# A decoder layer on one core: where three weight loads of its expert stage stand in SP's queue

## The chip, the cores and the metric

The kernel runs on one core of a Trainium2 chip. The metric is the device time of one execution in microseconds. A core has five engines with a queue each: TensorE (PE; its weight loads are shown as PEld), VectorE (DVE), ScalarE (ACT), GpSimd (POOL) and SyncE (SP), which here does nothing but wait and issue DMAs. Each queue is worked off in order: an instruction that waits on a semaphore holds all that stand behind it on its engine.

## The reference

A batch of 16 sequences of 112 rows of 256 numbers goes through three blocks, each with a residual and a layer norm behind it:

```
x = layernorm(x + ssm(x))        # projection to 512, short convolution, long convolution (FFT in the reference), gate, projection
x = layernorm(x + depool(x, ctx))# rms-norm and projection of x, plus a decayed sum over the first half of ctx
x = layernorm(x + moe(x))        # router: argmax of 8 logits; the chosen expert: relu(x W1.T + b1) W2.T + b2
```

Every row goes to one of eight experts. An expert's first weights W1 (256 x 1024) and its second weights W2 (1024 x 256) are 1 MB each in fp32. The kernel computes no expert that a row did not choose.

## The kernel before

**Stages.** Up to about 78 us the kernel projects, convolves and makes the long convolution's spectrum. From there until about 208 us runs a pipeline over the 16 sequences in 20 steps (`b_steps`: s = 2 * pair + q = 0 to 19). In step s every engine works on several sequences at different lags: `seq(pair, q, lag)` gives the sequence s - lag. Lag 0 loads ctx and x and transforms, lag 1 gates (VectorE) and inverts, lag 2 projects and adds the residual, lag 3 makes x1 and `cross` (the second block), lag 4 makes x2 (rows after the second block), stores it and computes the router's logits. Steps 16 to 19 are the tail in which no new sequence comes in. Behind the pipeline the expert stage runs over tiles of 128 rows sorted by expert, from about 226 us to the end.

**Early tiles.** Three tiles (`EARLY` = 3) don't wait for the whole routing. When the first ten sequences are routed, in step 15, VectorE finds which experts the first three full tiles belong to (`early_experts`, which sets `expert_e_set`) and which rows they hold (`early_tokens`). GpSimd then gathers their rows from `x2_early` with an indirect DMA (`gather_early`, L755): tile 0 in the middle of step 16, tiles 1 and 2 at that step's end. TensorE does the tiles' work between its other work: `turn_early(i)` (L1676) transposes the gathered rows; `hide_early(i, part)` (L1687) is the first product in two halves of 16 matmuls, which needs `w1_e_loaded`; ScalarE applies the relu (`relu_early`, L956); `sum_up_early(i, part)` (L1697) is the second product in two halves of 8 matmuls, which needs `w2_e_loaded` and counts `f_e_ps`. Its order is written by hand: in step 17 project(15), turn_x1(14), turn_x2(13), turn_early(0), cross(14), hide_early(0, 0), logit(13); in step 18 turn_x1(15), hide_early(0, 1), cross(15), sum_up_early(0, 0), turn_x2(14), sum_up_early(0, 1), logit(14), a ranking; in step 19 turn_x2(15), turn_early(1), logit(15), hide_early(1, 0). Tile 1's rest and all of tile 2 follow behind the steps, with the matmuls that place the rows of the main tiles (L1785) between them.

**Weights.** The early tiles have two buffers for either kind of weights: `w1_e` in the region of `w2`, `w2_e` at the start of `stage_b`, in the place of the first two chunks of the gate z, which are free when half the sequences are gated (`gate_set` at 8). Tile 2 uses tile 0's buffers again, so its loads wait until `ht_e_ps` is 2 (first product of tile 0 done) and `f_e_ps` is 1 (second product done). All experts' W1 are loaded into `w1` in 16 pieces of 512 KB: piece n by `load_w1(n, gates)`, which waits until `gates` sequences are gated, since the last pieces lie over the last z chunks. Pieces 0 to 12 go out in steps 0 to 12, pieces 13, 14 and 15 in steps 17, 18 and 19. W2 of experts 0 to 3 goes out in 16 pieces of 256 KB, W2 of experts 4 to 7 behind the steps (L569). `b2`, broadcast to all partitions (1 MB, L560), is needed by VectorE before it copies the first main tile's W1 (`take_w1`, L1400) .

**SP's queue.** All these loads are SP's. In each step it stores x2 of lag 4, loads a W2 piece of lag 1, does what the tail of the function asks, and loads ctx (L536) and x (L538) of lag 0. `load_early_w1` (L503) and `load_early_w2` (L508) first read the tile's expert into a register (`value_load`), then issue. In step 15 both of tile 0 stand last. In step 17 SP waits for all three gathers and then issues both of tile 1 and the next W1 piece. Behind the steps come tile 2's W1, b2, W2 of expert 7, tile 2's W2, and W2 of experts 5, 4 and 6, each with its own wait.

**Main tiles.** GpSimd gathers their rows from `x2_rows` (L788, the first four by 221 us), TensorE transposes them (L1798), ScalarE moves them (L1064), then come 32 matmuls with W1 (L1811) and 16 with W2 (L1830) per tile.

Of the kernel before, what the change touches and what calls it, by code (L numbers as in the profile page):

```python
# [25 lines left out]
NB, L, D = 16, 112, 256  # L26
H, MODES, TAPS = 512, 8, 4
C, PATCHES = 512, 375
NE, FF = 8, 1024
# [15 lines left out]
EARLY, EARLY_SEQS, EARLY_GROUP = 3, 10, 2  # L45
# [61 lines left out]
def need(engine, semaphore, value):  # L107

    if not (isinstance(value, int) and value <= 0):
        engine.wait_ge(semaphore, value)  # L110

def decoder_layer(nc, ins, out):
    at, _ = constant_columns()
    n_const = max(b for _, b in at.values())
    NLAG = LA + LO + 1

    with ExitStack() as ctx:
# [3 lines left out]
        def sem(name):  # L122
            return ctx.enter_context(nc.semaphore(name))
# [105 lines left out]
        def z_chunk(c):  # L229
# [4 lines left out]
        q = Region(stage_b[:, 2 * DT * FF:r.used], r.used - 2 * DT * FF)  # L234
# [18 lines left out]
        q = Region(stage_b[:, late:late + 1848], 1848)  # L253
# [111 lines left out]
        rows_e_loaded = [sem(f"rows_e_loaded{i}") for i in range(EARLY)]  # L365
        rt_e_ps, rt_e_set, ht_e_ps, ht_e_set, f_e_ps, sum_e_set = (
            sem(s) for s in ("rt_e_ps", "rt_e_set", "ht_e_ps", "ht_e_set", "f_e_ps", "sum_e_set"))
# [8 lines left out]
        def b_steps(engine, step):  # L376

            for s in range(NB + EPI):
                step(s // 2, s % 2)

        def seq(pair, q, lag):

            par, half = (q - lag) % 2, pair + (q - lag) // 2
            b = 2 * half + par
            if isinstance(b, int) and not 0 <= b < NB:
                return None, par, half
            return b, par, half
# [39 lines left out]
        def apart(engine, *waits):  # L427

            waits = [(s, v if isinstance(v, int) else engine.snap(v)) for s, v in waits]  # L430
            if not all(isinstance(v, int) for _, v in waits):
                engine.wait_ge(loaded["consts"], 16)
            for s, v in waits:
                need(engine, s, v)
# [25 lines left out]
        @block.sync  # L460
        def _(sp):
            sp.dma_start(lens, ins["lens"]).then_inc(loaded["lens"], 16)
            sp.dma_start(consts[:, 0:n_early], ins["consts"][:, 0:n_early]).then_inc(loaded["consts_early"], 16)

            def load_w_in(h):
                sp.dma_start(w_in[:, :, h * P:(h + 1) * P], ins["w_in"][:, :, h * P:(h + 1) * P])\
                  .then_inc(w_in_loaded[h], 16)

            def load_hid(c):
                sp.dma_start(hid_t[:, :, c * CW:(c + 1) * CW], ins["x_t"][:, :, c * CW:(c + 1) * CW])\  # L470
                  .then_inc(hid_loaded[c], 16)

            load_w_in(0)
            load_hid(0)
            for h in range(1, HT):
                load_w_in(h)
            sp.dma_start(w_in[:, :, H:2 * H], ins["w_in"][:, :, H:2 * H]).then_inc(loaded["w_in_z"], 16)
            for c in range(1, NC):
                load_hid(c)
            sp.dma_start(consts[:, n_early:], ins["consts"][:, n_early:]).then_inc(loaded["consts"], 16)  # L480
            sp.dma_start(w_out, ins["w_out"]).then_inc(loaded["w_out"], 16)
            for dst, name in ((w_x[:, :, :], "w_x"), (g_res[:, :], "g_res"), (w_r[:, :, :], "w_r"),
                              (b1[:, :], "b1"),
                              (u[L:L + 1, 0, :], "b_x"), (u[L:L + 1, 1, :], "b_x"),
                              (decay[L:L + 1, :], "one_row")):
                sp.dma_start(dst, ins[name]).then_inc(loaded["small"], 16)
            sp.dma_start(b_r[:, :], ins["b_r"].to_broadcast([L, NE])).then_inc(loaded["small"], 16)
            sp.dma_start(g_init[:, :], ins["g_init"].to_broadcast([L, D])).then_inc(loaded["small"], 16)

            sp.wait_ge(pad_set, 1)  # L490
            sp.dma_start(x2_rows[T:T + 1, :], pad_row).then_inc(loaded["pad"], 16)
            sp.dma_start(x2_early[EARLY_SEQS * L:EARLY_SEQS * L + 1, :], pad_row).then_inc(loaded["pad"], 16)
            def load_w1(n, gates):

                need(sp, gate_set, gates)
                sp.dma_start(w1[:, n // 2, n % 2, :], ins["w1"][:, n // 2, n % 2, :]).then_inc(loaded["w1"], 16)

            w2_pieces = ins["w2"].rearrange("p e m d -> p (e m d)")

            def load_early_w1(i):  # L500

                e = sp.value_load(expert_e[0:1, i:i + 1], min_val=0, max_val=NE - 1)
                sp.dma_start(w1_e[i % 2], ins["w1"][:, e, :, :]).then_inc(w1_e_loaded[i % 2], 16)  # L503

            def load_early_w2(i):

                e = sp.value_load(expert_e[0:1, i:i + 1], min_val=0, max_val=NE - 1)
                sp.dma_start(w2_e[i % 2], ins["w2"][:, e, :, :]).then_inc(w2_e_loaded[i % 2], 16)  # L508

            def step(pair, q):  # L510

                b, par, half = seq(pair, q, 4)
                if b is not None:
                    sp.wait_ge(x2_set, b + 1)
                    sp.dma_start(x2_rows[bass.ds(b * L, L), :], x2[:, par, :]).then_inc(x2_stored[par], 16)
                    if b < EARLY_SEQS:
                        sp.dma_start(x2_early[bass.ds(b * L, L), :], x2[:, par, :]).then_inc(early_stored[par], 16)

                b, par, half = seq(pair, q, 1)
                if b is not None:  # L520
                    sp.wait_ge(dft_ps, b + 1)
                    sp.dma_start(w2_flat[:, bass.ds(b * H, H)], w2_pieces[:, bass.ds(b * H, H)])\
                      .then_inc(loaded["w2"], 16)
                if 2 * pair + q == NB + 1:
                    for i in range(EARLY):
                        sp.wait_ge(rows_e_loaded[i], 16)
                    load_early_w1(1)
                    load_early_w2(1)
                if 2 * pair + q > NB:
                    load_w1(2 * pair + q - 4, NB)  # L530
                b, par, half = seq(pair, q, 0)
                if b is None:
                    return
                need(sp, u_set, b - 1)
                need(sp, sq_set, b - 1)
                sp.dma_start(ctx_sb[:, par, :], ins["ctx"][b, :, :]).then_inc(c_loaded[par], 16)  # L536
                need(sp, pre_set, b - 1)
                sp.dma_start(x_res[:, par, :], ins["x"][b, :, :]).then_inc(x_loaded[par], 16)  # L538
                if isinstance(b, int) and b == 0:
                    sp.wait_ge(spec_set, HT)  # L540
                    sp.wait_ge(xt_ps, HT * NC)
                    sp.wait_ge(loaded["pad"], 32)
                if b >= PRO:
                    sp.wait_ge(decay_set, 1)
                if b <= 12:
                    load_w1(b, 10 if b == 12 else 0)
                if b == NB - 1:
                    sp.wait_ge(expert_e_set, 1)
                    sp.wait_ge(gate_set, NB // 2)
                    sp.wait_ge(z_ps, UNITS)  # L550
                    load_early_w1(0)
                    load_early_w2(0)

            b_steps(sp, step)
            sp.wait_ge(out_ps, NB)
            sp.wait_ge(gate_set, NB)
            sp.wait_ge(cross_ps, NB)
            sp.wait_ge(ht_e_ps, 2)
            load_early_w1(2)
            sp.dma_start(shared[:, :], ins["b2"].to_broadcast([P, NE * D])).then_inc(loaded["b2"], 16)  # L560
            for e in (7, 5, 4, 6):
                if e == 5:
                    sp.wait_ge(f_e_ps, 1)
                    load_early_w2(2)
                if e in (4, 5):
                    sp.wait_ge(ht_e_ps, 6 if e == 4 else 4)
                if e == 6:
                    sp.wait_ge(rows_loaded[0], 16)
                sp.dma_start(w2[:, e, :, :], ins["w2"][:, e, :, :]).then_inc(loaded["w2"], 16)  # L569
# [1319 lines left out]
```

## Time and profile before

| | |
|---|---|
| median of three runs | 348.27 us (347.13 to 348.81) |
| the profiled execution | 348.85 us, span 347.0 us |
| TensorE busy | 324.0 us, 93% of the span |
| VectorE, GpSimd, ScalarE busy | 213.0, 200.3, 151.2 us |
| granted TensorE clock, mean | 0.981 of full |
| DMA | 42.43 MB, mean 122 GB/s |

A row of the timeline gives an instruction's start from the span's begin, its length, its engine, its line and what it writes and reads; a bracket gives the idle time of the engine before it and what ended that. The chain of the work that ended last gives, for each piece, the time for which it alone decided when the rest could go on: for a DMA it counts from the issue.
### The profile page before, as it was taken

The page shows a single profiled execution, that of the slowest core. Times are in us where ns is not written, and L with a number is a line of the kernel's source. Part 1 is how long each engine was busy: PE and PEld are TensorE (multiplying, and loading weights), DVE is VectorE, ACT ScalarE, POOL GpSimd, SP SyncE. Part 2 cuts the span into 40 slices and gives each one's busy share as a digit, 9 for nine tenths or more (in the row PEclk, how much of TensorE's full clock was granted, in tenths as well). Part 3 has the DMA queues.
Part 4 walks back from the last instruction along what each step waited for, and adds up shares of the span by engine and source line. Part 5 has one row for each costly group of instructions (what it writes and reads, how often), then busy time and mean ns, then how long its engine had stood idle before and what let it go on. Part 6 is the DMA issues. An engine that isn't in the chain of part 4 may idle for free.

```text
span 347.0 us, 6576 instructions
## 1 busy us (share of the span) xinstructions
PE 324.0 (93%) x1923; PEld 255.3 (74%) x1924; DVE 213.0 (61%) x497; ACT 151.2 (44%) x383; POOL 200.3 (58%) x325
## 2 busy tenths in 40 slices
PE   7999989999999999999996899889999999999970
PEld 2555555567777778777784788789999999999950
DVE  5999994625977788788886246543344444354431
ACT  3888864246543444443354333233432234422320
POOL 4689990335587685786867221412764565565552
PEclk9999999999999999999999699999999999999996
DMA  6910002503357665576338679940110101110120
GB/s 186 363 43 2 2 0 62 161 0 107 125 173 235 192 190 158 183 208 176 89 86 297 220 265 376 347 201 8 69 50 28 33 30 29 32 33 30 30 48 24
DMA packets 19999, 42.43 MB, mean 122 GB/s; under 512 B 3761, under 2 KB 10905, under 8 KB 18554
## 3 DMA queue, kind: packets, MB, share of 16 engines
q1 hardware_dynamic: 17370, 37.32, 32.8%
q0 software_dynamic: 1872, 4.59, 4.7%
q8 instruction: 17, 0.28, 0.4%
q14 instruction: 20, 0.16, 0.2%
q10 hardware_dynamic: 720, 0.08, 0.2%
HBM read 37.16 MB, written 5.34 MB: 122 GB/s over the span
## 4 chain that ended last, share of the span: by engine, by line
PE 72%; DVE 14%; DMA 6%; POOL 2%; issue 2%; ACT 1%; SPq 1%; ACTq 1%; DVEq 0%; POOLq 0%
PE ps L1811 16%; PE ps L1830 15%; DVE stage_b L1126 9%; PE ps L1609 7%; PE ps L1631 7%; PE ps L1498 5%; PE ps L1547 4%; PE ps L1654 4%; DMA stage_b<-in_w 4%; PE ps L1548 4%; DMA early<-x_early,early 2%; PE ps L1658 2%; PE ps L1687 1%; PE ps L1697 1%; PE ps L1666 1%
## 5 line engine op out<-in xcount | busy, mean ns | idle before, releaser
L1811 PEld LDWEIGHTS ps<-stage_b 128*128 128x128 f32 x480 | 55.8, 192 | 2.3 <-issue 1.6
L1811 PE MATMUL ps<-stage_b 128*128 128x128 f32 x480 | 56.2, 275 | 1.2 <-ACT stage_b L1064 1.2
L1830 PE MATMUL ps<-w,stage_b 128*128 x240 | 54.4, 380 | 0.9 <-DVE stage_b L1437 0.9
L1830 PEld LDWEIGHTS ps<-w,stage_b 128*128 128x128 f32 x240 | 44.4, 190 | 6.7 <-issue 1.3
L1278 DVE TENSOR_TENSOR stage_b<-ps,w 112x512 f32<-112x512 f32 x64 | 39.7, 682 | 13.6 <-PE ps L1548 11.5
L718 POOL TENSOR_TENSOR stage_b<-stage_b 112x512 f32<-112x512 f32 x16 | 21.4, 1336 | 37.8 <-DVE stage_b L1278 25.6
L1609 PEld LDWEIGHTS ps<-consts,stage_b 112*128 112x128 f32 x256 | 31.0, 192 | 7.3 <-issue 6.6
L1055 ACT ACTIVATE stage_b<-ps,b 128x128 f32<-128x128 f32 x120 | 32.7, 383 | 5.6 <-issue 5.6
L1064 ACT ACTIVATE stage_b<-ps 128x256 f32<-128x256 f32 x16 | 6.1, 384 | 65.8 <-PE ps L1798 65.8
L788 POOL DMA_INDIRECT stage_b<-x_rows,stage_b x18 | 28.3, 1571 | 7.3 <-issue 5.2
L1126 DVE SCALAR_TENSOR_TENSOR stage_b<-ps,w,stage_b 128x444 f32<-128x444 f32 (+2 forms) x48 | 31.1, 671 | 1.1
L1609 PE MATMUL ps<-consts,stage_b 112*128 112x112 f32 x256 | 31.1, 274 | 0.1
L1631 PE MATMUL ps<-w,stage_b 128*112 128x256 f32 x128 | 30.3, 380 | 0.0
L1400 DVE COPY stage_b<-w 128x2048 f32 x16 | 19.8, 1238 | 15.0 <-issue 11.4
L1461 PE MATMUL ps<-w 128*128 128x448 f32 x64 | 26.6, 543 | 0.9 <-DMA w<-in_x_t 0.9
L966 ACT ACTIVATE stage_b<-stage_b 112x256 f32<-112x256 f32 x16 | 9.6, 599 | 40.5 <-POOL stage_b L737 40.5
L1498 PE MATMUL ps<-w 128*128 128x448 f32 x64 | 26.7, 544 | 0.0
L1437 DVE TENSOR_TENSOR stage_b<-ps,shared 128x256 f32<-128x256 f32 x15 | 6.4, 424 | 29.6 <-PE ps L1830 28.9
L1631 PEld LDWEIGHTS ps<-w,stage_b 128*112 128x112 f32 x128 | 21.3, 177 | 3.8
L719 POOL TENSOR_TENSOR stage_b<-stage_b 112x512 f32<-112x512 f32 x16 | 20.7, 1292 | 0.0
L834 POOL DMA_INDIRECT out<-stage_b x15 | 15.8, 1052 | 8.4 <-POOL stage_b L831 8.4
L1165 DVE TENSOR_SCALAR stage_b<-stage_b 128x256 f32<-128x256 f32 x15 | 6.2, 412 | 21.4 <-POOL stage_b L829 21.4
(217 smaller groups left out, 599.4 us busy)
## 6 DMA issues: line engine op xcount, KB each, us to landing
w<-in_w SPq DMA_DIRECT2D x16, 512.0 KB, 4.5
w<-in_w SPq DMA_DIRECT2D x7, 1024.0 KB, 4.8
w<-in_w SPq DMA_DIRECT2D x16, 256.0 KB
stage_b<-in_ctx SPq DMA_DIRECT2D x16, 224.0 KB, 3.1
stage_b<-in_w SPq DMA_DIRECT2D x3, 1024.0 KB, 7.3
w<-in_x_t SPq DMA_DIRECT2D x4, 448.0 KB, 6.3
stage_b<-in_x SPq DMA_DIRECT2D x16, 112.0 KB, 2.9
x_rows<-stage_b SPq DMA_DIRECT2D x16, 112.0 KB
```

The source lines that it names most:

```text
L718: g.tensor_tensor(y_spec[:, 0, :], prod[:, 0, :], prod[:, 1, :], ALU.subtract)
L719: g.tensor_tensor(y_spec[:, 1, :], prod[:, 2, :], prod[:, 3, :], ALU.add).then_inc(y_set, 1)
L788: g.indirect_dma_start(rows[:, place, :], None, x2_rows, bass.IndirectOffsetOnAxis(ap=index, axis=0)).then_inc(rows_loaded[place], 16)
L1055: last = a.activation(h_t[:, par, m * P:(m + 1) * P], ps[:, 2 * par + m // 4, (m % 4) * P:(m % 4 + 1) * P], ACT.Relu, bias=b1[:, bass.ds(e ...
L1126: ins_ = v.scalar_tensor_tensor(acc[:, :, back:L], raw[:, :, 0:L - back], conv_w[:, h, tap:tap + 1], acc[:, :, back:L], ALU.mult, ALU.add)
L1278: last = v.tensor_tensor(prod[:, n, :], ps[0:L, x_part, :], spec[:, k_part, :], ALU.mult)
L1461: last_ = m.matmul(ps[:, h, 0:CW], w_in[:, k, h * P:(h + 1) * P], hid_t[:, k, bass.ds(c * CW, CW)], start=(k == 0), stop=(k == DT - 1))
L1498: last_ = m.matmul(ps[:, z_bank(unit), 0:CW], w_in[:, k, H + unit % HT * P:H + (unit % HT + 1) * P], hid_t[:, k, unit // HT * CW:(unit // ...
L1609: last_ = m.matmul(ps[:, 3, h * L:(h + 1) * L], y_spec[:, s, h * P:(h + 1) * P], const(name, L), start=(s == 0), stop=(s == 1))
L1631: last_ = m.matmul(ps[0:L, 4, 0:D], gated[:, par, h * L:(h + 1) * L], w_out[:, h, :], start=(h == 0), stop=(h == HT - 1))
L1811: last_ = m.matmul(ps[:, 2 * par + f // 4, (f % 4) * P:(f % 4 + 1) * P], w1_now[par][:, k, f * P:(f + 1) * P], rows_t[:, par, k * P:(k + 1 ...
L1830: last_ = m.matmul(ps[:, 4 + par, 0:D], h_t[:, par, f * P:(f + 1) * P], w2[:, e, f, :], start=(f == 0), stop=(f == FT - 1))
```

## The change

Three things in SP's queue, and nothing on another engine.

- The second weights of early tile 0 no longer go out in step 15, right behind its first weights. They go out in step 16, behind the W2 piece, after a wait until tile 0's gather has landed. In step 17 SP accordingly waits for the gathers of tiles 1 and 2 only.
- Pieces 13 and 14 of W1 go out in steps 14 and 15, behind the W2 piece and ahead of ctx, with waits until 12 and 14 sequences are gated. In step 17 only piece 15 is left.
- Behind the steps, the second weights of tile 2 go out right behind its first weights, ahead of b2 and of W2 of expert 7; before, both stood ahead of them.

```diff
--- before.py
+++ after.py
@@ -521,13 +521,17 @@
                     sp.wait_ge(dft_ps, b + 1)
                     sp.dma_start(w2_flat[:, bass.ds(b * H, H)], w2_pieces[:, bass.ds(b * H, H)])\
                       .then_inc(loaded["w2"], 16)
+                    if 13 <= b < 15:
+                        load_w1(b, 2 * (b - 7))
+                if 2 * pair + q == NB:
+                    sp.wait_ge(rows_e_loaded[0], 16)
+                    load_early_w2(0)
                 if 2 * pair + q == NB + 1:
-                    for i in range(EARLY):
+                    for i in range(1, EARLY):
                         sp.wait_ge(rows_e_loaded[i], 16)
                     load_early_w1(1)
                     load_early_w2(1)
-                if 2 * pair + q > NB:
-                    load_w1(2 * pair + q - 4, NB)
+                    load_w1(2 * NE - 1, NB)
                 b, par, half = seq(pair, q, 0)
                 if b is None:
                     return
@@ -549,7 +553,6 @@
                     sp.wait_ge(gate_set, NB // 2)
                     sp.wait_ge(z_ps, UNITS)
                     load_early_w1(0)
-                    load_early_w2(0)
 
             b_steps(sp, step)
             sp.wait_ge(out_ps, NB)
@@ -557,11 +560,10 @@
             sp.wait_ge(cross_ps, NB)
             sp.wait_ge(ht_e_ps, 2)
             load_early_w1(2)
+            sp.wait_ge(f_e_ps, 1)
+            load_early_w2(2)
             sp.dma_start(shared[:, :], ins["b2"].to_broadcast([P, NE * D])).then_inc(loaded["b2"], 16)
             for e in (7, 5, 4, 6):
-                if e == 5:
-                    sp.wait_ge(f_e_ps, 1)
-                    load_early_w2(2)
                 if e in (4, 5):
                     sp.wait_ge(ht_e_ps, 6 if e == 4 else 4)
                 if e == 6:
```

## Rows read from the trace of the kernel before

**Rows 1.** The page: its first line and the chain by engine.
```profile
span 347.0 us, 6576 instructions
...
PE 72%; DVE 14%; DMA 6%; POOL 2%; issue 2%; ACT 1%; SPq 1%; ACTq 1%; DVEq 0%; POOLq 0%
```

**Rows 2.** The chain that ended last, in order: start us, us, what.
```profile
184.56 7.48 DMA early<-x_early,early
...
192.78 1.71 PE ps L1654 x4
194.49 0.85 PE ps L1658 x2
195.34 2.85 PE ps L1687 x16
...
198.74 1.80 PE ps L1687 x16
200.54 0.86 PE ps L1654 x4
...
208.67 12.97 DMA stage_b<-in_w
```

**Rows 3.** TensorE in time: start, us, line, operation, count [idle before <-releaser].
```profile
189.06 0.41 PE L1642 MATMUL ps<-consts,stage_b 112*128 112x112 f32 x2 [0.75 <-ACT stage_b L1039]
192.09 0.69 PE L1676 MATMUL ps<-consts,early 128*128 128x128 f32 x2 [2.62 <-DMA early<-x_early,early]
...
221.69 3.72 PE L1697 MATMUL ps<-stage_b 128*128 128x256 f32 x16 [1.73 <-DMA stage_b<-in_w]
```

**Rows 4.** Stretches: length, busy us (count) of five engines, TensorE clock, DMA share, GB/s.
```profile
188.00:190.00 2.00, 0.72 (x4) 0.30 (x4) 0.36 (x2) 1.80 (x5) 1.44 (x4) 1.00 0.98 345
190.00:192.00 2.00, 0.00 (x0) 0.00 (x0) 0.00 (x0) 0.00 (x0) 1.79 (x4) 0.66 0.87 316
220.00:222.00 2.00, 0.32 (x1) 0.30 (x2) 1.58 (x5) 1.14 (x4) 1.46 (x3) 1.00 1.08 416
```

**Rows 5.** SP in time: its DMA issues around the change.
```profile
176.79 0.31 SPq L536 DMA_DIRECT2D stage_b<-in_ctx  x1
...
182.39 0.38 SPq L503 DMA_DIRECT2D w<-in_w  x1
183.54 0.36 SPq L508 DMA_DIRECT2D stage_b<-in_w  x1
...
194.34 0.34 SPq L503 DMA_DIRECT2D w<-in_w  x1
...
206.61 0.35 SPq L503 DMA_DIRECT2D w<-in_w  x1
...
208.67 0.35 SPq L508 DMA_DIRECT2D stage_b<-in_w  x1
```

**Rows 6.** Landings of L503, of L755 (without its first), of L788, in this order.
```profile
DMA to landing us min/median/max: 4.6/4.8/6.8
...
DMA to landing us min/median/max: 3.6/4.2/4.7
...
DMA to landing us min/median/max: 3.6/4.0/7.8
```

**Rows 7.** GpSimd in time: the third early gather, r1, the first main gather.
```profile
189.92 0.95 POOL L755 DMA_INDIRECT early<-x_early,early  x1 [0.30 <-issue]
...
192.00 0.26 POOL L737 TENSOR_SCALAR stage_b<-stage_b 112x2 f32<-112x2 f32 x1
...
216.10 1.09 POOL L788 DMA_INDIRECT stage_b<-x_rows,stage_b  x1 [1.88 <-DVE stage_b L1383]
```

**Rows 8.** ScalarE in time: the ctx square of sequence 15, a relu of tile 2.
```profile
182.12 0.61 ACT L981 ACTIVATE stage_b<-stage_b 112x512 bf16<-112x512 f32 x1
...
220.60 1.14 ACT L956 ACTIVATE stage_b<-ps,b 128x128 f32<-128x128 f32 x4 [1.15 <-PE ps L1687]
```

**Rows 9.** VectorE in time: the first copy of a main tile's first weights.
```profile
218.21 1.27 DVE L1400 COPY stage_b<-w 128x2048 f32 x1 [1.05 <-issue]
```

## The prediction

> **What bounds the kernel now.** The profiled execution took 348.85 us for a span of 347.0 [rows 1], so 1.85 us lie around the span; the median of the three runs is 348.27, 0.58 below it. I take the saving from the span and subtract it from the median. I read four views in this order. First the chain that ended last: TensorE holds 72% of it, and only two of its pieces behind the start are transfers: the gather of early tile 0's rows, 7.48 us from its issue at 184.56, and the load of early tile 2's second weights, 12.97 us from 208.67 [rows 2]. Second, TensorE in order of time, to see how much of each transfer it really waits: 2.62 us ahead of the turn of tile 0's rows at 192.09, and 1.73 us ahead of tile 2's second product at 221.69 [rows 3]. Most of either transfer is hidden; the two idle pieces are what a better order can give. Third, the stretches: TensorE's clock was 1.00 (2.4 GHz) from 188 to 190 and 0.66 from 190 to 192, while it stood idle [rows 4]. The chain shows what followed: four matmuls of `cross` took 1.71 us where they take 0.86 eight microseconds on, the next two 0.85, half a first product of an early tile 2.85 against 1.80 [rows 2]. So the wait is paid twice, once as idleness and once as 1.2 GHz. Fourth, SP's queue and the landings, for who can be early.
>
> **Part 1: tile 0's second weights load behind its gather.** Before, SP issued the first weights at 182.39 and the second at 183.54, 1 MB each, and the gather followed at 184.56 [rows 5, 2]. It took 7.48 us; the next two gathers, the second issued at 189.92, when that traffic was running out, took 3.6 to 4.7, and the main gathers have a median of 4.0 [rows 6, 7]. From 184 on the engines moved about 345 GB/s [rows 4]. Ahead of the gather's end stood 1.05 (first weights) + 1.05 (second) + 0.115 (x2 store) + 0.262 (w2 piece) + 0.131 (the gather) = 2.61 MB, 7.6 us at that rate, from about 183.9 (1.5 us behind the first issue) to 191.5; the trace has 192.04. Without the second weights 1.56 MB remain, 4.5 us, so it ends at 188.4, and with the same 0.5 us of excess at 188.9. The shortest gather, 3.6 us, gives 188.2 [rows 6]. TensorE reaches the turn when the two transposes at 189.06, 0.41 us long, are through, at 189.47 [rows 3]. So the gather stops being awaited: 2.62 us saved, with 0.6 to 1.3 us in hand. Bounds: 0 if the gather stays at 7.48, 2.62 if it lands by 189.47; no gain beyond that, since the transposes ahead of it wait for ScalarE.
>
> The clock: the two short idle pieces before 189.47 stay, but they stood there with the clock at 1.00, and a 1.73 us wait later left 220 to 222 at 1.00 too, with TensorE busy 0.32 of 2 us [rows 3, 4]. I therefore take the clock to stay up. The saving is (1.71 - 0.86) + (2.85 - 1.80) = 1.90, and half of what ran at half clock and has no twin here, 0.85 and the turn's 0.69: 0.77. In all 2.67 us; bounds 0 and 2.67.
>
> What is late next: x1 of sequence 15 waits for GpSimd's r1 at 192.00 + 0.26 [rows 7] and one ScalarE pass of 0.6, so its turn can start at 192.9. In the shifted order TensorE needs it at 189.47 + 0.3 + 0.86 + 0.43 + 1.80 + 0.2 = 193.1. That just fits: 0 to 0.3 us lost, 0.1 taken.
>
> Then the moved load itself. SP waits until 188.9, needs 0.8 us to read the expert (the gap of 1.15 us between its issues at 182.39 and 183.54 less the first one's 0.38), and issues at 189.7. With a landing of 4.8 us for the shortest loads of this size, plus 0.26 MB of gathers in the same stretch (0.8 us), it lands at 195.3 [rows 5, 6]. It is first used behind the second `cross`, which ended at 200.54 + 0.86 + 0.43 = 201.8, in the new time 201.8 - 5.2 = 196.6 [rows 2]. 1.3 us in hand; cost 0. Its range is a landing of 4.6 to 12.97 us, 194.3 to 202.7, so 0 to 6.1 us.
>
> Queued behind SP's new wait are the x2 store of sequence 13 (its buffer is next wanted for sequence 15, two steps on), then the waits for gathers 1 and 2 and tile 1's weights. Gather 2, issued 189.92, now shares its time with the moved 1 MB: 4.7 + half of 2.9 = about 6, so 195.9 instead of 193.6, and tile 1's first weights go out at 196.6 instead of 194.34 and land at 201.4 [rows 5 to 7]. TensorE wants them at 207.4 before, 202.2 now. 0.8 us in hand; I take 0.2 us for it, range 0 to 3.
>
> **Part 2: two pieces of the late first weights in steps 14 and 15.** 512 KB each go out ahead of the ctx load of their step, on gates that VectorE set a step earlier. Each costs SP one issue of about 0.4 us and ctx about 0.52/0.345 = 1.5 us. The ctx load issued at 176.79 would land at 181.9 if I give it the 3.6 us of the shortest transfer in rows 6 and the piece ahead; ScalarE squares it at 182.12 [rows 5, 6, 8]. 0.2 us in hand: cost 0, range 0 to 1. What they take away are two of three such pieces from 194 to 206, 1.05 MB of traffic or 3 us of the queue. This covers the extra megabyte that Part 1 moves there.
>
> **Part 3: tile 2's second weights ahead of b2 and w2[7].** Before: first weights 206.61, b2, w2[7], second weights 208.67, landed 221.64 [rows 5, 2]. Now their wait (tile 0's product done) is met before 206.6, so they are second in line instead of fourth: 2.1 MB less ahead, 5 to 6 us. The wait of 1.73 us goes. What is late next is ScalarE's second half of the relu, 220.60 + 1.14 = 221.74 before [rows 8]; TensorE is free at 219.96 (221.69 less its wait), and the first half of the 3.72 us product takes it to 221.8 as well. Saving 1.7 us; bounds 0 and 1.8. The price is b2, one megabyte (2.9 us) later; VectorE's first weight copy at 218.21 stands behind it [rows 9]. It ends at 219.5 and is wanted when the product of 221.69 is through, 225.4 before and, on the same axis, 223.7 now, so 4.2 us cover it. The main tiles' first gather, issued at 216.10 into a full queue [rows 7], has landed by about 223 (an estimate from its 6.8 us; the longest of these is 7.8 [rows 6]) and was wanted at 225.4. Shifted by 5.2 it lands at 217.7 to 218.7 and is wanted at 218.5: 0 to 0.2 us lost, 0.1 taken.
>
> The main tiles behind are TensorE's own work, one product after the other, and shift as they are.
>
> **Sum.** 2.62 + 2.67 + 1.7 = 6.99, less 0.1 + 0.2 + 0.1: 6.6 us. 348.27 - 6.6 = 341.7 us (the profiled execution: 342.3).
>
> The row against which a rule can be held is the 7.48 us gather [rows 2]. The Trainium skill ("DMA: Bandwidth & Descriptors", Queues, rings and completion order) says that each DMA engine takes turns between the queues it has work for, a packet at a time. By that rule the gather, on its own queue, would hardly stand behind SP's second megabyte, and taking it away would win little; the sum would be Part 3 alone, 346.6. The same section says that a semaphore's increment lands only after the earlier writes of its engine in all queues, which fits the row.
>
> **Rivals.** (a) The gather is late anyway: it reads rows just stored and takes 7.48 for a reason other than the queue. For: it is the first of its kind, and it overlaps the first weights too. Against: 3.6 to 4.7 for the next two, 7.8 only where the queue is full again. Part 1 gives nothing: 348.27 - 1.7 = 346.6. (b) The clock falls nonetheless, on the short idle pieces before 189.47 (one of 0.75 us, one like it). Against: it had not fallen by 190. 6.6 - 2.67 = 3.9 saved, 344.4. (c) SP's wait makes tile 1's weights late. If gather 2 takes 7.5 us, it lands at 197.4, the first weights go out at 198.2 and land at 203.0 to 205.0, and TensorE idles 0.8 to 2.8 us: 1.6 more than I charge, 343.3; with the clock down as well 345.9. (d) Slower: the moved load is late itself. TensorE stands ahead of tile 0's second product, in the middle of the last steps, with the turn of x2 14 behind it. With the 12.97 us of the third such load it would land at 202.7, 6.1 us late, and 2.7 more go to the clock: 6.6 - 8.8 = 2.2 slower, 350.5. It decides from a landing at 200.5, 10.8 us behind the issue. For: that row. Against: that load had some 3 MB ahead of it, this one has 0.26.
>
> **How the numbers follow.** Forecast 0.66, with its own range 340.5 to 343.2; (a) 0.09, (b) 0.08, (c) 0.12, (d) 0.03, something unforeseen 0.02. The range 340.4 to 345.4 leaves out (a), (d), the clock case of (c) and the tails of the forecast, about 2 in 10. About 0.5% (1.7 us) is what can be told from no change. (a) lies on that bound and is shared between same and faster: faster 0.90, same 0.06, slower 0.04.
>
> **What would show it.** Right: the gather at 184.56 lands before 189.4; L1676 has no idle time; the clock is 1.00 from 186 to 235; L1687's first half 1.8 us; the second weights are issued near 189.7; L1697 at about 215 follows L1687 without a DMA as releaser; the first L1811 starts near 219.5. Wrong: the gather over 5 us, the clock below 1 after 190, or a DMA as the releaser of L1687 or L1697.

## The result, and the profile after

The changed kernel takes 344.64 us (343.41 to 345.29, 4 runs) against 348.23 (347.13 to 348.81): 3.6 us less, ratio 0.9889, interval 0.9852 to 0.9925. Run again over five rounds it takes 342.60 against 348.33, ratio 0.9851 (0.9815 to 0.9887). The ratios leave out the slow executions, and they can differ by up to 0.003 from the quotient of the two medians. The forecast was 341.7, its range 340.4 to 345.4: the first median is 2.9 us above the forecast and inside the range.

The profiled execution has a span of 343.4 us, 3.6 less than before. First the chain that ended last, of the changed kernel; these rows answer to [rows 2].

```profile
186.09 5.26 DMA early<-x_early,early
...
191.39 0.69 PE ps L1678 x2
192.08 1.71 PE ps L1656 x4
193.79 0.85 PE ps L1660 x2
194.64 1.94 PE ps L1689 x16
...
197.13 1.80 PE ps L1689 x16
198.93 0.86 PE ps L1656 x4
...
218.36 3.46 PE ps L1699 x16
...
222.66 3.81 PE ps L1813 x32
```

The gather takes 5.26 us instead of 7.48. No load stands in the chain behind it: the 12.97 us piece ahead of tile 2's second product is gone. But `cross` still takes 1.71 us, as before, and the half of the first product behind it 1.94, where it was 2.85 before and the other half takes 1.80: TensorE ran at half clock again, for a shorter time. The stretches, with TensorE's, its loads', VectorE's, ScalarE's and GpSimd's busy us, the clock, the DMA share and GB/s, show when; they answer to [rows 4].

```profile
188.00:190.00 2.00, 1.20 (x6) 0.54 (x4) 1.30 (x4) 1.17 (x3) 1.61 (x5) 1.00 0.70 266
190.00:192.00 2.00, 1.02 (x5) 0.81 (x6) 0.00 (x0) 1.38 (x4) 1.65 (x2) 0.86 0.17 42
192.00:194.00 2.00, 2.00 (x6) 1.43 (x5) 0.00 (x0) 0.58 (x2) 1.57 (x4) 0.50 0.55 115
194.00:196.00 2.00, 2.00 (x15) 1.90 (x14) 1.03 (x3) 1.18 (x3) 0.14 (x1) 0.79 0.96 387
```

TensorE in order of time shows what is left of the two waits of [rows 3].

```profile
190.57 0.41 PE L1644 MATMUL ps<-consts,stage_b 112*128 112x112 f32 x2 [0.74 <-ACT stage_b L1041]
191.39 0.69 PE L1678 MATMUL ps<-consts,early 128*128 128x128 f32 x2 [0.41 <-DMA early<-x_early,early]
...
218.19 3.62 PE L1699 MATMUL ps<-stage_b 128*128 128x256 f32 x16
```

2.62 us became 0.41 and 1.73 became nothing. From the gather's issue to the first product of the main tiles it was 226.25 - 184.56 = 41.69 us and is 222.66 - 186.09 = 36.57: 5.12 us gained. Of these 2.2 are the idleness ahead of the turn (7.53 to 5.30 us behind the issue) and 2.0 lie at tile 2's second product: its wait of 1.73 and 0.26 of the product behind it (3.72 against 3.46 in the chain). The remaining 0.9 is the clock: from the turn to tile 1's first product it was 15.31 us before and is 14.40 now, and 12.76 in the profile of the changed kernel below in which the clock stayed up, so 2.6 were lost before and 1.6 now. The span shows only 3.6, since the gather was issued 1.53 us later than before. That delay is from the kernel's first matmuls, which the change does not touch. TensorE in time, before and then after:

```profile
7.21 3.27 PE L1461 MATMUL ps<-w 128*128 128x448 f32 x8 [0.92 <-DMA w<-in_x_t]
...
7.05 4.97 PE L1463 MATMUL ps<-w 128*128 128x448 f32 x8 [1.98 <-DMA w<-in_x_t]
```

The same eight matmuls took 1.70 us longer, and this is the clock once more: from 8 to 10 us it was 1.00 before and 0.50 here. In the repeated profile of the same kernel they take 3.27 again and the gather's issue is at 184.22, earlier than before's. The change has no part in it, and the time from the gather's issue to the first main product leaves it out. This measure is used below for every profile, beside the times.

### The profile page after: what moved, and what is told of

Read it like the earlier page. It is cut to its first block, busy times and chain, and to the rows that moved or that the text cites. A ratio compares the mean times of both kernels' runs of the same rounds, so it can differ in the third digit from the quotient of the medians.

```text
span 343.4 us, 6576 instructions
## 1 busy us (share of the span) xinstructions
PE 323.3 (94%) x1923; PEld 255.1 (74%) x1924; DVE 213.0 (62%) x497; ACT 151.1 (44%) x383; POOL 199.9 (58%) x325
## 4 chain that ended last, share of the span: by engine, by line
PE 78%; DVE 11%; DMA 4%; ACT 2%; POOL 2%; issue 1%; SPq 0%; DVEq 0%; POOLq 0%; ACTq 0%
PE ps L1813 16%; PE ps L1832 14%; DVE stage_b L1128 8%; PE ps L1611 7%; PE ps L1633 7%; PE ps L1500 5%; PE ps L1549 4%; PE ps L1656 4%; PE ps L1550 4%; PE ps L1689 3%; PE ps L1699 3%; PE ps L1660 2%; DMA early<-x_early,early 2%; PE ps L1463 1%; DMA w<-in_x_t 1%; PE ps L1668 1%
## 5 line engine op out<-in xcount | busy, mean ns | idle before, releaser
L1463 PE MATMUL ps<-w 128*128 128x448 f32 x64 | 28.3, 572 | 2.0 <-DMA w<-in_x_t 2.0
L1500 PE MATMUL ps<-w 128*128 128x448 f32 x64 | 26.7, 544 | 0.0
```

The costliest lines, as they stand in the source:

```text
L1463: last_ = m.matmul(ps[:, h, 0:CW], w_in[:, k, h * P:(h + 1) * P], hid_t[:, k, bass.ds(c * CW, CW)], start=(k == 0), stop=(k == DT - 1))
L1500: last_ = m.matmul(ps[:, z_bank(unit), 0:CW], w_in[:, k, H + unit % HT * P:H + (unit % HT + 1) * P], hid_t[:, k, unit // HT * CW:(unit // ...
```

## The experiments

| kernel | ratio (95%) | issue to first main product, gain |
|---|---|---|
| changed, first measurement | 0.9889 (0.9852 to 0.9925) | 36.57 us, 5.1 |
| changed, again | 0.9851 (0.9815 to 0.9887) | 35.07, 6.6 |
| part 3 alone (e1) | 0.9974 (0.9946 to 1.0003) | 39.11, 2.6 |
| part 1 alone (e2) | 0.9973 (0.9937 to 1.0010) | 37.09, 4.6 |
| part 2 alone (e3) | 0.9959 (0.9931 to 0.9986) | 39.73, 2.0 |
| before, pauses filled (e6) | 0.9925 (0.9892 to 0.9959) | 43.00, -1.3 |
| changed, pauses filled (e5) | 0.9841 (0.9791 to 0.9891) | 34.87, 6.8 |
| changed, w2 piece behind (e4) | 0.9825 (0.9770 to 0.9880) | 34.66, 7.0 |
| changed, first weights behind too (e9) | one run, 345.50 us | 38.62, 3.1 |
| without part 2 (e8) | 0.9842 (0.9786 to 0.9899) | 36.49, 5.2 |
| without part 3 (e10) | 0.9866 (0.9809 to 0.9923) | 37.11, 4.6 |
| e4 and piece 15 last (e11) | 0.9799 (0.9747 to 0.9850) | 34.43, 7.3 |
| e11, pauses filled (e12) | 0.9787 (0.9738 to 0.9836) | 34.43, 7.3 |

The kernel before spread over 346.3 to 352.1 us in these rounds, so half a per cent between two of these kernels is not told apart by their times; the right column is one execution each. Changed again and e1 to e3 ran on one chip, e4, e5, e6 and e9 on a second, e8 and e10 to e12 on a third, each beside the kernel before.

**The changed kernel again.**

> The changed kernel once more, beside its parts. Theory: from the gather's issue on it gains 5.1 us (2.2 of idleness ahead of L1678, 1.0 of the clock, 1.8 of the second product of tile 2), and the 1.5 us by which its start was longer in the first profile is chance: over five rounds it comes out 4.5 to 5.2 us faster (ratio 0.985 to 0.987). Rival: the later start belongs to the change; then 3.3 to 3.9 us (0.989 to 0.9905).

Within the stated times. This execution went as the forecast had it. TensorE in time:

```profile
189.01 0.44 PE L1678 MATMUL ps<-consts,early 128*128 128x128 f32 x2
189.28 1.06 PE L1656 MATMUL ps<-w_x,stage_b 128*112 128x256 f32 x4
190.61 1.95 PE L1689 MATMUL ps<-stage_b,w 128*128 128x128 f32 x16
...
209.81 0.57 PE L1787 MATMUL ps<-stage_b,w 112*128 112x42 bf16 x16 [0.48 <-POOL stage_b L778]
```

The gather landed in 4.7 us, before L1678 wanted it, nothing waited, the clock stayed at 1.00 and `cross` and the first product ran at full speed. 5.3 us were gained up to tile 1's first product (17.55 us behind the gather's issue, 22.84 before); then 0.65 was given back, at a place that the forecast did not name. VectorE shows it:

```profile
206.53 0.17 DVE L1369 TENSOR_SCALAR stage_b<-ps 128x8 f32<-128x8 f32 x1 [1.07 <-DMA x_rows<-stage_b]
```

Before it computes the main tiles' rows, VectorE waits for the store of the last x2. With everything 5 us earlier, that store stands behind tile 1's two loads and piece 15 in SP's queue; with piece 15 behind the store (e11, below) the wait is gone.

**Its three parts alone.** Part 3: only the tail's order, as in the change's last two hunks. Part 1: only

```diff
                     load_early_w1(0)
-                    load_early_w2(0)
...
+                if 2 * pair + q == NB:
+                    sp.wait_ge(rows_e_loaded[0], 16)
+                    load_early_w2(0)
                 if 2 * pair + q == NB + 1:
-                    for i in range(EARLY):
+                    for i in range(1, EARLY):
```

and part 2: only the lines with `load_w1`.

> Only part 3: tile 2's second weights ahead of b2 and of W2 of expert 7. Theory: the parts add up, and this one is worth its wait of 1.73 us: 1.6 to 1.9 us faster (0.9945 to 0.9955), the gather unchanged at about 7.5 us and the clock at half from about 191 to 196. Rival: the queue of that stretch is full whatever the order, and w2[7] or the main gather becomes late instead: under 0.8 us.

> Only part 1: tile 0's second weights behind its gather, with the first weights' pieces 13 to 15 and the tail order as before. Theory: the gather lands in about 5.3 us, L1676 waits 0.4 us and the clock still falls for some 4 us: 3.2 us faster (0.990 to 0.992). If part 2 is needed to make room for the moved megabyte, tile 1's weights or L1697 wait here and it is under 2.5 us.

> Only part 2: pieces 13 and 14 of the first weights in steps 14 and 15. Theory: nothing waits for these pieces and ctx lands in time, so same time within 0.4 us (0.999 to 1.001). Rival: they clear the queue for tile 2's second weights (which would then land earlier, since less traffic stands before 206) and bring up to 1 us, or they delay ctx of sequence 15 and cost up to 1 us.

Part 3's trace is as expected (tile 2's second product follows the first with no wait); its time has room for the expected 1.6 us, but for nothing as well. The other two theories failed. Part 2 is worth 1.4 us, not nothing: its rival, the queue cleared for tile 2's second weights, is what came, and for more than the 1 us that I gave it. Here is TensorE in time with part 2 alone, tile 2's second product:

```profile
218.11 3.81 PE L1689 MATMUL ps<-stage_b,w 128*128 128x128 f32 x32 [0.52 <-issue]
221.75 3.62 PE L1699 MATMUL ps<-stage_b 128*128 128x256 f32 x16
```

The 1.73 us wait is gone although tile 2's weights still stand fourth in line. So parts 2 and 3 remove the same wait, and I had credited it to part 3 only. Part 1 alone came out 0.9 us faster, an interval that includes no change, where its profile has 4.6; its runs spread from 343.95 to 352.15. In the profiled execution, the fastest of them, TensorE in time still has the other wait:

```profile
189.80 0.44 PE L1678 MATMUL ps<-consts,early 128*128 128x128 f32 x2 [0.65 <-DMA early<-x_early,early]
190.07 1.03 PE L1656 MATMUL ps<-w_x,stage_b 128*112 128x256 f32 x4
...
216.78 3.72 PE L1699 MATMUL ps<-stage_b 128*128 128x256 f32 x16 [1.69 <-DMA stage_b<-in_w]
```

What this kernel's other executions wait for, no profile shows. The times of the three parts (0.9, 0.9 and 1.4 us) add up to less than the whole change gained, the profiles (2.6, 4.6 and 2.0) to more than it did. That parts 2 and 3 overlap is shown by the wait that either removes, not by the times.

**The clock by itself.** In both kernels constants are multiplied in TensorE's pauses ahead of the turn of tile 0; their results are not used and overwritten.

```diff
+            def keep_busy(n):
+                pe.wait_ge(prod_set, NB)
+                for _ in range(n):
+                    m.matmul(ps[:, 0, :].rearrange("p (r n) -> p r n", r=4), ones16[:, :], filler, start=True, stop=True)
...
                     project(NB - 1)
+                    keep_busy(2)
                     turn_x1(NB - 2)
+                    keep_busy(3)
                     turn_x2(NB - 3)
+                    keep_busy(11)      # 1 in the changed kernel
                     turn_early(0)
```

> The kernel before, with 16 matmuls of constants (128x512, bf16, results not used) in TensorE's three pauses ahead of the turn of tile 0: two, three and eleven. No transfer changes, so the gather still takes 7.5 us and L1676 still starts 7.5 us behind its issue. Theory: the clock falls only because TensorE stands idle; kept busy it stays at 1.00, cross takes 0.86 and the first half product 1.80, and the kernel is 2.6 to 2.8 us faster (0.992 to 0.9925) with the wait itself still there. Rival: the clock falls for another reason, or the turn starts late behind the fillers: no gain or slower.

> The changed kernel with six such matmuls in the same three pauses (two, three and one; together 1.3 of the 1.8 us of idleness). Theory: the short pauses together with the 0.4 us wait are what lets the clock fall; filled, it stays at 1.00, cross 0.86, first half product 1.80: 1.6 to 1.8 us faster than the changed kernel, so 6.2 to 6.9 us against before (0.980 to 0.982). Rival: the clock level is decided further back, gain under 0.5 us over the changed kernel.

Before, filled, is 0.75% faster, 2.6 us (0.9892 to 0.9959), as expected, with no transfer moved and the gather at 7.52 us. TensorE in time of this kernel:

```profile
189.36 2.54 PE L1683 MATMUL ps<-ones 128*128 128x512 bf16 x11
192.19 0.44 PE L1676 MATMUL ps<-consts,early 128*128 128x128 f32 x2 [0.29 <-DMA early<-x_early,early]
192.47 1.03 PE L1654 MATMUL ps<-w_x,stage_b 128*112 128x256 f32 x4
193.77 1.95 PE L1693 MATMUL ps<-stage_b,w 128*128 128x128 f32 x16
...
221.38 5.41 PE L1703 MATMUL ps<-stage_b 128*128 128x256 f32 x16 [3.90 <-DMA stage_b<-in_w]
```

The turn starts no earlier, but behind it everything runs at full speed: tile 1's first product starts 12.73 us behind the turn, 15.31 before. That is the clock's share of the wait, measured alone, 2.6 us. The last row is why this one execution, at 350.27 us above its kernel's median of 346.59, was no faster: tile 2's weights, issued at 206.34, 2.3 us earlier than before, landed 15 us later, at 221.34, where they had landed at 221.64 before, and the product behind them took 5.41 us, not 3.72. When TensorE comes earlier the tail's loads become the bound; parts 2 and 3 are for this. In the changed kernel the fillers kept the clock at 1.00 too, but the expected 1.6 to 1.8 us over the unfilled one did not come: 0.9841 is not to be told from 0.9851. The profile of the unfilled one had the clock at 1.00 as well the second time.

**What the gather's length depends on.** One kernel moves the last 256 KB piece of the second weights behind the gather too, the other tile 0's first weights.

```diff
                     sp.wait_ge(dft_ps, b + 1)
+                    if b == NB - 1:
+                        sp.wait_ge(rows_e_loaded[0], 16)
+                        load_early_w2(0)
                     sp.dma_start(w2_flat...
```

```diff
                     sp.wait_ge(z_ps, UNITS)
-                    load_early_w1(0)
...
                     sp.wait_ge(rows_e_loaded[0], 16)
+                    load_early_w1(0)
                     load_early_w2(0)
```

> The changed kernel with the last 256 KB piece of the second weights also behind the gather. Theory: the gather lands when what stands ahead of it in the queues has drained, so it comes 0.5 to 0.7 us earlier (4.6 us), the 0.41 us wait of L1678 goes, and the clock falls less or not at all: 0.4 us faster than the changed kernel, up to 2.2 if the clock stays up. Rival: the gather takes 5.3 us for reasons of its own (its 128 rows, the x2 store): same time as the changed kernel.

> The changed kernel with tile 0's first weights behind the gather as well, so that only the x2 store and one 256 KB piece are in flight with it. Theory: the gather lands in 3.6 to 3.9 us; then TensorE waits for the first weights instead (issued at about 190.5, landed at 195 or later, wanted at 191) and the kernel is slower than the changed one. Rival: the gather's length does not come from SP's traffic: still about 5.2 us.

Without the first weights the chain reads

```profile
184.29 3.07 DMA early<-x_early,early
...
188.33 4.77 DMA w<-in_w
```

So the gather takes 3.07 us with 0.4 MB of SP's in flight, 3.4 to 4.5 with the first weights and the store (e4, e11, e12), 4.2 to 5.5 with the 256 KB piece besides (the changed kernel, e2, e5, e8, e10), and 7.05 to 7.52 with both megabytes (before, e1, e3, e6). It grows with what SP has ahead of it, though the two middle groups overlap; a reason of its own, my rival (a), is out.

The two later gathers show how late a load can still hold one up. In ten cases SP issued a megabyte of weights shortly behind such a gather's issue. Where it did so 0.8 to 1.3 us behind, the gather took 2.8 to 3.7 us (e2, e5, e11, e12), 0.65 us behind, 4.0 and 4.1 (the changed kernel, e10), and 0.1 to 0.3 us behind, 5.2 to 6.1 (changed again, e4, e8, e9). GpSimd is busy with the issue for 0.95 to 1.08 us, so such a load may still get ahead of part of the gather; that reason is not shown.

As expected, the kernel that moves both now waits for the first weights, 2.30 us (345.5 us, one run, which does not order it by time). The piece moved behind takes the gather off TensorE's path, at 3.4 us where 4.6 was expected, and has the lowest ratio of the single edits to the changed kernel, though not clear of it.

**Without part 2, without part 3.** The change less the `load_w1` lines, and the change less the tail's hunks.

> The change without part 2 (pieces 13 to 15 of the first weights in steps 17 to 19 as before). Theory: either part 2 or part 3 alone takes the 1.7 us wait of tile 2's second product away, but behind part 1 the queue of 195 to 215 is full, so the megabyte of the two pieces comes back as late landings: the x2 store of sequence 15 or tile 2's weights are waited for 0.5 to 2 us more than in the changed kernel, 3.0 to 4.7 us faster than before (0.9865 to 0.9915), and scattered. Rival: part 3 alone is enough, same time as the changed kernel (0.985).

> The change without part 3 (tile 2's second weights behind b2 and W2 of expert 7 as before). Theory: with tiles coming 5 us earlier, two megabytes more ahead of this load make L1699 wait 1 us or more: 3.0 to 4.3 us faster than before (0.9875 to 0.9915). Rival: the pieces out of the way are enough, as they were alone; same time as the changed kernel (0.985).

Without part 2 the time is the rival's, without part 3 it lies between theory and rival; in either case part 1 with one other part is within the scatter of the whole change. Both profiled executions gained less than the changed kernel's second one. Tile 2's second product starts 0.3 us late in the one without part 3 (3.92 us behind its first, against 3.64), not the 1 us or more of the theory. And in both the clock fell. In the one without part 2 the turn started 0.49 us behind the transposes ahead of it, against 0.31 in the changed kernel's second profile: its weight load had waited for the gather (the first row below). The stretches show the clock at half right behind it, with TensorE busy throughout:

```profile
189.21 0.20 PEld L1677 LDWEIGHTS ps<-consts,early 128*128 128x128 f32 x2 [0.29 <-DMA early<-x_early,early]
...
188.00:190.00 2.00, 1.20 (x6) 0.85 (x7) 0.05 (x1) 1.77 (x5) 1.53 (x3) 0.99 0.06 19
190.00:192.00 2.00, 2.00 (x7) 1.51 (x6) 0.00 (x0) 0.11 (x2) 1.72 (x4) 0.50 0.79 174
192.00:194.00 2.00, 2.00 (x14) 2.00 (x14) 1.03 (x3) 1.33 (x3) 0.73 (x2) 0.66 0.95 393
```

**Both late pieces moved.** The piece behind the gather, and piece 15 of the first weights behind the last x2 store, in step 19; then the same with two and three fillers.

```diff
                     load_early_w2(1)
-                    load_w1(2 * NE - 1, NB)
+                if 2 * pair + q == NB + 3:
+                    load_w1(2 * NE - 1, NB)
```

> The changed kernel with the last 256 KB piece of the second weights behind the gather and piece 15 of the first weights in step 19, behind the x2 store of sequence 15. Theory: the wait of L1369 for that store (0.7 to 1.1 us, half of it passed on to TensorE) goes, L1678 waits for no gather: 0.4 to 0.7 us faster than the changed kernel (0.980 to 0.984). Rival: piece 15 now delays tile 2's weights, no gain.

> The same with two and three matmuls of constants in TensorE's pauses of 0.6 and 0.7 us ahead of the turn of tile 0. Theory: where the clock falls in some executions only, this keeps it up in all: median 0 to 1 us below the one without, the slowest executions gone. Rival: with the gather no longer waited for the clock never falls, and the two are the same.

Both times lie close to what was expected. No wait for the store is left in either, the clock stayed at 1.00 in both, and both reach the first main product 34.43 us behind the gather's issue, so what the fillers add there is not shown: the longest runs are 343.35 and 343.11 us. The last has the lowest ratio of all, 341.83 us (341.26 to 343.11) against 349.03, and is clearly faster than before; that it is faster than the changed kernel (0.9738 to 0.9836 and 0.9815 to 0.9887, on other chips) is likely, not shown.

## Why the prediction was right, and where it was off

**The gather.** Right in mechanism: the second megabyte held it up. Forecast 3.6 to 4.3 us, off TensorE's path by 0.6 to 1.3 us; measured 5.26, 0.41 us on the path, in the first profile, and 4.7, off the path, in the second. My sum from bytes and 345 GB/s was too short by 0.9 us or more in the first profile, and the 0.6 us in hand did not cover it. Of the prediction's own signs of being wrong, two showed in the first profile: the gather over 5 us, and the clock below 1 after 190. From the Trainium skill's account ("DMA: Bandwidth & Descriptors", Queues, rings and completion order), that an engine takes turns between queues, I had worked out that the gather would hardly be held up; the runs disagree with that reading: from 3.07 to 7.5 us it follows SP's traffic. Whether it waits for the data or only for its semaphore behind the other queue's writes, no run here separates.

**The clock.** The mis-sized term. I gave it 2.67 us and set the risk of its falling at 0.08, with the argument that it had stood at 1.00 by 190 and had survived 1.73 us of idleness later. The second profile gives 2.6, the first only 0.9. The two pauses of about 0.64 and 0.75 us are still there, and in three of the seven profiles that had no longer wait the clock fell: with a wait for the gather of 0.41 us (the changed kernel), of 0.42 (without part 3), and of 0.29 at the weight load alone (without part 2). It stayed up with 0.65 (part 1 alone) and in the three with no such wait (changed again, e4, e11). In all three profiles with filled pauses it stayed up. So the two pauses by themselves, rival (b), never brought it down here; with a short wait behind them they did in three of four. Four and three profiles are few, so this is a pattern and not a rule. That a later pause of 1.73 us passed said nothing about these. The median of 344.64 is close to rival (b)'s 344.4 by luck: its profile lost 1.6 us to the clock and 1.5 to the kernel's start.

**Part 3.** Forecast 1.7 us, measured 2.0 with what follows the wait, and wrongly attributed: part 2 alone gives it too. I had seen the 3 us that the pieces free in the queue and used it only as cover for Part 1's megabyte.

**What was late next.** x1 of sequence 15 was no limit, and the moved load landed in time. Tile 1's weights went out 10.1 and 11.9 us behind the first gather's issue (forecast 12.0) and were not waited for: rivals (c) and (d) did not occur in either profile. The third gather took 5.7 us in the second profile, where I had 6. What came instead was the last x2 store, 0.65 us in the second profile, behind the loads that I had costed one by one for TensorE but not for VectorE.

**The sum.** 6.6 us forecast; 6.6 from the gather's issue in the second profile, by 5.3 + 2.0 - 0.65. That they meet is partly luck: the 0.4 us that I charged for small losses did not occur where I put them, 0.65 came at another place, and tile 2's second product gave 0.3 more than forecast. In time it was 3.6 in the first measurement and 5.2 (0.9851) in the second, both inside the range and both short of 6.6. The first profile shows two causes of such a shortfall, the clock behind the gather and the clock at the kernel's start; how often either comes, few profiles can't say.

## What to carry to other kernels

Where a transfer is waited for, look at what its queue neighbours were issued for: a megabyte first used some 18 us after its issue cost here 2.6 us of wait and 2.6 of clock. A wait of TensorE is to be priced with what runs behind it, and a forecast that the clock stays up wants the pauses around it filled or gone, not only the long one. And parts that drain the same queue can remove the same wait: test each alone, and look in its trace for the wait that is gone, before crediting it.

## What the runs showed that I had not expected

The clock's fall isn't settled by the length of the last wait alone: 0.65 us ahead of L1678 left it at 1.00 (part 1 alone), while 0.29 at its weight load let it drop to 0.50 from 190 to 192 (without part 2). And 16 useless matmuls made the kernel before faster by 2.6 us (0.9925) without moving any transfer. The kernel's start, up to the gather's issue, takes 184.2 to 184.6 us in eleven profiles and 185.00, 186.09 and 186.49 in three. In the last two (the changed kernel and e3) the clock fell at the start: TensorE had waited 1.98 and 1.90 us ahead of L1463, whose eight matmuls took 4.97 us, not 3.27. With a wait of 1.81 (e2) they took 3.27.
